# Second cross attention: the maxima are turned in fp32, and split into high and low part behind the turning, out of PSUM

## The reference

```python
x = x + _L0_attn_ref(_layernorm(x), ...)
x = x + _L0_xattn_ref(_layernorm(x), ctx_1024, fside_SxS2_0, ...)
x = x + _L0_ffn_ref(_layernorm(x), ...)
x = x + _L1_attn_ref(_layernorm(x), ...)
x = x + _L1_xattn_ref(_layernorm(x), ctx_1024, ctx_1024, ...)
x = x + _L1_ffn_ref(_layernorm(x), ...)
```

## Time and profile before

| | us |
|---|---|
| median of 3 runs | 1443.18 (1441.4 to 1446.35) |
| the profiled execution | 1440.46 |
| its span, first to last instruction | 1438.7 |
| granted TensorE clock over the span | 0.980 |
| batches 2 to 13 of the second cross attention | 26.95 each |

### The profile page before, as it was taken

One profiled execution on the slowest core, in us unless ns is written; L12 is line 12 of the kernel. 1 busy time (PEld: TensorE's weight loads), 2 busy tenths in 40 slices (PEclk: granted clock), 3 DMA queues, 4 the chain that ended last, 5 costly groups with the idle time before them and its releaser, 6 DMA issues.

```text
span 1438.7 us, 25389 instructions
## 1 busy us (share of the span) xinstructions
PE 1356.1 (94%) x9210; PEld 1010.9 (70%) x9210; DVE 1051.1 (73%) x2115; ACT 863.1 (60%) x1849; POOL 790.3 (55%) x442
## 2 busy tenths in 40 slices
PE   7889999999999999999999977999999999996898
PEld 4648888888888888888857654565565565553687
DVE  6558777888887788877735678677777777771687
ACT  4437666676766676666614444666666666653575
POOL 5036444433444444441452280788888888898363
PEclk9999999999999999999998999999999999998899
DMA  3122222221111222221230314463453463410231
GB/s 84 62 89 53 55 57 57 56 57 45 38 47 48 57 57 55 53 56 35 82 111 25 87 23 107 109 142 96 108 142 97 110 141 95 90 42 1 86 103 47
DMA packets 71803, 104.39 MB, mean 73 GB/s; under 512 B 14670, under 2 KB 54934, under 8 KB 71550
## 3 DMA queue, kind: packets, MB, share of 16 engines
q1 hardware_dynamic: 60062, 91.39, 25.4%
q10 hardware_dynamic: 11616, 11.38, 2.8%
HBM read 63.65 MB, written 2.11 MB: 46 GB/s over the span
## 4 chain that ended last, share of the span: by engine, by line
PE 80%; DVE 10%; DMA 3%; POOL 2%; ACT 2%; issue 2%; SPq 1%; ACTq 0%; POOLq 0%; DVEq 0%
PE PS L701 9%; PE PS L1100 6%; PE PS L715 6%; PE PS L689 5%; PE PS L690 5%; PE PS L691 5%; PE PS L717 5%; PE PS L716 5%; PE PS L1114 5%; PE PS L1080 5%; PE PS L1039 3%; PE PS L1045 3%; POOL QO_area L1220 2%; PE PS L1731 2%; DMA inv_kept<-row_inv 2%; DVE QO_area L1386 2%
## 5 line engine op out<-in xcount | busy, mean ns | idle before, releaser
L1220 POOL TENSOR_TENSOR QO_area<-QO_area,prob_a 125x896 f32<-125x896 f32 x160 | 335.8, 2098 | 24.1 <-ACT prob_a L1312 3.2
L867 ACT ACTIVATE HL<-PS 125x512 fp32r<-125x512 f32 (+1 forms) x384 | 206.6, 539 | 178.4 <-PE PS L701 161.2
L959 DVE TENSOR_TENSOR HL<-PS,HL 125x512 fp32r<-125x512 f32 (+1 forms) x384 | 238.1, 622 | 74.8 <-ACT HL L867 54.1
L1386 DVE TENSOR_REDUCE QO_area<-PS 112x1 f32<-112x500 f32 x384 | 239.1, 671 | 59.9 <-PE PS L1080 59.6
L1312 ACT ACTIVATE prob_a<-PS 125x448 f32<-125x448 f32 x384 | 187.5, 540 | 105.9 <-PE PS L1100 100.8
L774 POOL TENSOR_TENSOR HL<-ctx_area,ones 125x512 fp32r<-125x512 f32 (+1 forms) x64 | 93.0, 1453 | 246.7 <-PE PS L717 193.6
L715 PE MATMUL PS<-HL 125*128 125x512 f32 (+1 forms) x384 | 155.7, 405 | 2.5 <-DVE HL L959 1.7
L689 PE MATMUL PS<-HL 128*128 128x500 f32 x336 | 153.2, 456 | 4.1 <-DVE HL L929 4.0
L1100 PEld LDWEIGHTS PS<-HL 98*125 98x125 f32 x768 | 102.5, 186 | 71.9 <-ACT prob_a L1312 38.8
L877 ACT ACTIVATE prob_a<-prob_a,neg_max 128x500 f32<-128x500 f32 x192 | 135.5, 706 | 26.2 <-DVE neg_max L951 24.9
L1100 PE MATMUL PS<-HL 98*125 98x256 f32 x768 | 144.2, 309 | 1.6 <-ACT prob_a L1312 1.6
(11 more groups left out here) (260 smaller groups left out, 2729.3 us busy)
## 6 DMA issues: line engine op xcount, KB each, us to landing
HL<-prob_b SPq DMA_DIRECT2D x128, 187.5 KB, 4.0
ctx_area<-in_ctx_T SPq DMA_DIRECT2D x16, 750.0 KB, 13.0
ctx_area<-in_ctx SPq DMA_DIRECT2D x16, 750.0 KB
HL<-ctx_area SPq DMA_DIRECT2D x64, 187.5 KB, 3.8
inv_area<-in_ctx_T SPq DMA_DIRECT2D x8, 750.0 KB, 4.3
prob_a<-in_ctx_T SPq DMA_DIRECT2D x8, 750.0 KB, 4.6
inv_area<-inv_kept ACTq DMA_DIRECT2D x16, 256.0 KB, 3.3
ctx_area<-in_L_ffn_W SPq DMA_DIRECT2D x16, 256.0 KB, 3.2
```

Source lines behind the costliest of these rows:

```text
L867: nc.scalar.activation(pH[k % 3][0:KC, 0:width(g)], PS[0:KC, 2 + k % 3, 0:width(g)], ACT.Copy)\
L959: nc.vector.tensor_tensor(pL[k % 3][0:KC, 0:width(g)], PS[0:KC, 2 + k % 3, 0:width(g)], pH[k % 3][0:KC, 0:width(g)].bitcast(fp32), ALU.sub ...
L1220: nc.gpsimd.tensor_tensor(late_acc[b % 2], before, late_p[n % LATE_P], ALU.add).then_inc(m["padd"], 1)
L1386: nc.vector.tensor_reduce(late_part[b % 2][:, u // NKB, u % NKB:u % NKB + 1], PS[0:2 * S, u % NKB, 0:KB], AX, ALU.max).then_inc(m["mx"], 1)
```

## The change

`late_nmHL` goes, and with it the rounding and the subtraction ahead of the turning (lines 1395 and 1396). The fp32 maxima (112 x 8) are turned as they are, in step c = 0 instead of c = 1. ScalarE copies the turned 8 x 112 out of PSUM, rounded to fp32r, in step c = 0: this is the high row, and its DMA is issued there (`send_maxima(b, 0)`). In step c = 1, behind its two reductions, VectorE subtracts this high row from the PSUM original (`low_maxima`), and ScalarE, which waits for that (`nmlow`), issues the DMA of the low row behind its exponentials of c = 1. The key product of c = 2, which overwrites bank 7, waits for `nmlow` instead of `nmcopy`. The diff, without file names and unchanged neighbours:

```diff
         late_wq = carve(128, 4 * 3 * QUAD).rearrange("p (j r c) -> p j r c", j=4, r=3)
         late_nm = [carve(2 * S, 8) for i in range(2)]
         late_part = [carve(2 * S, 8 * NKB).rearrange("p (s w) -> p s w", s=8) for i in range(2)]
-        late_nmHL = [carve(2 * S, 16).bitcast(fp32r) for i in range(2)]
-        late_nmT = [carve(16, 2 * S).bitcast(fp32r) for i in range(2)]
+        late_nmT = [[carve(8, 2 * S).bitcast(fp32r) for r in range(2)] for i in range(2)]
         late_inv = [carve(128, 4 * S) for i in range(2)]
         late_p = [prob0[0:KC, i * HQ:(i + 1) * HQ] for i in range(LATE_P)]
         late_acc = [carve(KC, HQ) for i in range(2)]
...
         ld_k = [sem("ld_k0")]
         ld_late = [sem(f"ld_late{i}") for i in range(2)]
 
-        names = ("wqrep qp qhi qlo q0set qset ones kmm khi klo stack vmm vev mxmm mx nmsplit nmtr nmcopy nmrow "
+        names = ("wqrep qp qhi qlo q0set qset ones kmm khi klo stack vmm vev mxmm mx nmsplit nmtr nmcopy nmlow nmrow "
                  "sc exp pv padd sum norm wo out").split()
         la = {n: sem(f"late_{n}") for n in names}
         ld_v = sem("ld_v")
...
 
                 if piece == 0:
                     if b >= 2:
-                        pe.wait_ge(m["nmcopy"], b - 1)
+                        pe.wait_ge(m["nmlow"], b - 1)
                 elif piece < 4:
                     pe.wait_ge(m["khi"], 3 * b + piece)
                     pe.wait_ge(m["klo"], 3 * b + piece)
...
 
                 pe.wait_ge(m["nmsplit"], b + 1)
                 pe.wait_ge(m["vev"], 3 * min(b + 2, B))
-                nc.tensor.transpose(PS[0:16, 7, 0:2 * S], late_nmHL[b % 2].bitcast(fp32),
+                nc.tensor.transpose(PS[0:8, 7, 0:2 * S], late_nm[b % 2],
                                     ident[0:2 * S, 0:2 * S]).then_inc(m["nmtr"], 1)
 
             def scores(b, c, half):
...
                         project(b + 2, c - 2)
                     if b + 2 < B and c in (6, 8, 10):
                         project(b + 2, c // 2)
-                    if c == 1 and 0 <= b < B:
+                    if c == 0 and 0 <= b < B:
                         turn_maxima(b)
                     if 1 <= n:
                         product((n - 1) // NC, (n - 1) % NC)
...
                 act.wait_ge(m["nmtr"], b + 1)
                 if b >= 2:
                     act.wait_ge(m["nmrow"], 2 * 16 * (b - 1))
-                nc.scalar.activation(late_nmT[b % 2], PS[0:16, 7, 0:2 * S], ACT.Copy).then_inc(m["nmcopy"], 1)
+                nc.scalar.activation(late_nmT[b % 2][0], PS[0:8, 7, 0:2 * S], ACT.Copy).then_inc(m["nmcopy"], 1)
                 act.wait_ge(m["nmcopy"], b + 1)
                 act.wait_ge(m["ones"], 1)
                 if b >= 3:
                     act.wait_ge(m["sc"], 2 * NC * (b - 2))
-                for r in range(2):
-                    act.dma_start(
-                        late_q[b % 3].bitcast(fp32)[3 * QUAD + r:3 * QUAD + r + 1, 0:HQ],
-                        late_nmT[b % 2].bitcast(fp32)[8 * r:8 * r + 8, :]).then_inc(m["nmrow"], 16)
+                send_maxima(b, 0)
+
+            def send_maxima(b, r):
+
+                if r:
+                    act.wait_ge(m["nmlow"], b + 1)
+                act.dma_start(
+                    late_q[b % 3].bitcast(fp32)[3 * QUAD + r:3 * QUAD + r + 1, 0:HQ],
+                    late_nmT[b % 2][r].bitcast(fp32)).then_inc(m["nmrow"], 16)
 
             def first_keys():
                 for piece in range(3):
...
                         values(b + 2, c // 2 - 3, 7)
                     if b + 2 < B and c == 5:
                         queries(b + 2)
+                    if c == 0 and 0 <= b < B:
+                        place_maxima(b)
                     if c == 1 and 0 <= b < B:
-                        place_maxima(b)
+                        send_maxima(b, 1)
                 nc.scalar.preload_act_table(ACT.Sqrt)
 
             return first_keys, rest
...
                 dve.wait_ge(m["mx"], NKB * 8 * (b + 1))
                 if b >= 2:
                     dve.wait_ge(m["nmtr"], b - 1)
-                hl = late_nmHL[b % 2]
-                nc.vector.tensor_reduce(late_nm[b % 2], late_part[b % 2], AX, ALU.max, negate=True)
-                chain.link(dve, nc.vector.tensor_reduce(hl[:, 0:8], late_part[b % 2], AX, ALU.max, negate=True))
-                nc.vector.tensor_tensor(hl[:, 8:16], late_nm[b % 2], hl[:, 0:8].bitcast(fp32), ALU.subtract)\
+                nc.vector.tensor_reduce(late_nm[b % 2], late_part[b % 2], AX, ALU.max, negate=True)\
                     .then_inc(m["nmsplit"], 1)
+
+            def low_maxima(b):
+
+                dve.wait_ge(m["nmcopy"], b + 1)
+                if b >= 2:
+                    dve.wait_ge(m["nmrow"], 2 * 16 * (b - 1))
+                nc.vector.tensor_tensor(late_nmT[b % 2][1], PS[0:8, 7, 0:2 * S], late_nmT[b % 2][0].bitcast(fp32),
+                                        ALU.subtract).then_inc(m["nmlow"], 1)
 
             def normalise(b):
                 dve.wait_ge(m["sum"], b + 1)
...
                     if b + 1 < B:
                         maxima(b + 1, 2 * c)
                         maxima(b + 1, 2 * c + 1)
+                    if c == 1 and 0 <= b < B:
+                        low_maxima(b)
                     if b + 2 < B and c in (2, 3, 4):
                         keys(b + 2, c - 2, 7)
                     if n >= NC and n % NC == 3:
```

## The result

The changed kernel takes 1435.04 us, median of 8 runs (1431.6 to 1440.53), against 1444.24 us for the kernel before, median of 8 (1441.4 to 1449.36): ratio 0.9934, with a 95% interval of 0.9917 to 0.9951. By the ratio that is 9.5 us less (7.1 to 12.0), between the two medians 9.2 us; 6.9 us were forecast. The predicted time, 1436.3 us, is 1.3 us off. The profiled execution has a span of 1435.0 us at a mean clock of 0.975.

A forecast was written before the change was run, and what follows sets the result against it. TensorE bounds the kernel, stalled once a batch by VectorE's subtraction; GpSimd binds the end from batch 13. 12 x (1.07 - 0.43) = 7.7, less 0.5 and 0.3, is 6.9 us: 1443.18 to 1436.3 us, range 1430.5 to 1443.5.

The forecast's parts named there:

- Part 1: Steps c = 0 and c = 1: removing the subtraction ahead of the turning cuts 4.45 to 3.38 us, gaining 1.07 a batch.
- Part 2: VectorE's added 8 x 112 subtraction out of PSUM: 0.28 us, the middle of 0.18 and 0.391 us.
- Part 3: ScalarE's copy and first DMA issue moved from c = 1 to c = 0: exponentials 0.3 us late, cost nothing.
- Part 4: ScalarE's wait for nmlow before the second DMA issue delays TensorE's key product at c = 3: 0.43 us lost a batch.
- done at s + 0.94: Low row subtraction's end, in us after step c = 2 starts (s): reductions end s + 0.62, gap 0.04, subtraction 0.28.
- Part 5: Batches 0 and 1: batch 0 loses 0.5 us by the key product's wait; batch 1 gains nothing and loses 0.3 us.
- The end: From batch 13's first addition GpSimd runs 33 additions back to back, 2.227 us each; only gains before that move the end.
- The sum: Whole kernel: 12 x (1.07 - 0.43) = 7.7 us, less 0.5 and 0.3, gives 6.9 us gained.
- the rivals: Four other outcomes: wait at c = 3 takes nearly all (0.16), wait hidden (0.10), contention (0.07), stall stays (0.07).
- The slower one: VectorE behind c = 1's reductions: new subtraction waits for GpSimd, 1.83 us; 11.7 us slower, 1455 us; chance 0.07.

The follow-up runs named there:

- e1: The kernel before with the subtraction of line 1396 replaced by a third reduction, so the low row holds the high row again; ratio 0.9909.
- e2: The changed kernel run again without an edit, on the chip of e1, e3 and e4; ratio 0.9931 to the kernel before.
- e7: The changed kernel with the low row subtracted from an fp32 copy in SBUF, made by ScalarE, instead of out of PSUM; ratio 1.0041 to the kernel before.
- e5: The changed kernel with ScalarE's low row wait and second DMA issue moved behind the key copy of c = 2; ratio 0.9906 to the kernel before.
- e6: The changed kernel plus an unused 112 x 8 subtraction with two SBUF inputs at the old one's place on VectorE; ratio 1.0036 to the kernel before.
- e8: The changed kernel with the low row's subtraction done twice in a row; a single time, 1438.31 us.
- e4: e3 with the last batch's 11 additions done by VectorE instead of GpSimd; ratio 0.9874 to the kernel before.
- e3: The changed kernel with both DMAs of the maxima rows issued by SyncE instead of ScalarE; ratio 0.9905 to the kernel before.
- e9: e3 with the low row subtracted one step earlier, behind c = 0, in batch 0 alone; ratio 0.9901 to the kernel before.
- e10: e4 with batch 14's column sums and normalising moved behind all work of batch 15; ratio 0.9845 to the kernel before.

## Why the prediction was right

- *Part 1, the gain at c = 0 and c = 1:* 1.07 us forecast, 4.45 - 3.37 = 1.08 measured, and e1 gives the same from the instruction alone.
- *Part 2, the new subtraction:* 0.28 us forecast, 0.25 measured.
- *Part 3, ScalarE's copy and first issue at c = 0:* at no cost, and so it is. The exponentials of c = 1 started 0.73 us behind their scores instead of 0.54 (1003.88 for 1003.15), which nobody waited for.
- *Part 4, the wait for the low row:* the mechanism as forecast, step by step, and its size off: 0.43 us forecast, 0.28 measured (4.02 - 3.74), 0.25 in batch 4 alone (4.01 - 3.76). The term mis-sized is "done at s + 0.94": it was done at s + 0.79. I had let the subtraction begin a gap of 0.04 us behind the reductions' recorded end, but it begins 0.08 us ahead of it (1005.33, where the pair that starts at 1004.15 ends 1.26 us later), as the records of VectorE's instructions overlap there; the rest is the 0.03 us of the subtraction.
- *Part 5:* batch 1 cost 0.4 us (interval of the first additions 26.18 before, 26.59 after), 0.3 forecast. Batch 0 cost 1.6 instead of 0.5: the wait of 0.49 us was right, the clock under it was not foreseen.
- *The end:* 73.5 us from batch 13's first addition on, in every kernel with GpSimd's 33 additions, whatever was done to the batches before. This held exactly.
- *The sum:* 12 x 0.80 = 9.6 us, less 0.4 and 1.6, gives 7.6 us by the traces, where 6.9 were forecast; measured over all runs are 9.5 us (7.1 to 12.0), an interval that holds the 7.6 near its lower end. Two errors of mine, 12 x 0.16 = 1.9 us too little gain and 1.2 too little loss, partly cancel. That the predicted time is only 1.3 us off is partly luck too: it was counted from a median before of 1443.18 us, and that of all 8 runs is 1.06 us higher. Between profiled executions the time ahead of the stage, where nothing was changed, differs by up to 7 us (first split at 891.27 in e2, 898.72 in e7), so a single pair of spans (1438.7 and 1435.0) says less than the stage's own intervals.

Of the rivals, none happened. The slower one was real as a mechanism (e7) and did not apply as the operand lies in PSUM.

## What to carry to other kernels

A tiny VectorE instruction that takes ten times its time, and not always, is waiting for somebody: look at how many of its inputs lie in SBUF and at what GpSimd does beside it, and see whether one of them can be read from PSUM. When work is moved off the path, follow the new wait to the engine's next work: here a wait and an issue of ScalarE ahead of the exponentials of c = 2 gave 0.3 us of 1.1 back, and the same two behind the key copy (e5) cost nothing. And look how far a gain can travel: what is saved after the point where another engine has no idle time left does not arrive at the end.

## What the runs showed of the hardware

- A 112 x 8 subtraction with two SBUF inputs took 1915 ns on average beside GpSimd's additions of 2.10 us (e6), an 8 x 112 one 1181 ns (e7), and with one input in PSUM 253 to 257 ns (the change, e8). In batch 0, without additions, the first two took 159 and 254 ns. In the kernel before such a subtraction ended 0.02 to 0.04 us behind the end of an addition, in 15 batches of 15.
- VectorE's additions of 125 x 896 with two SBUF inputs hold up GpSimd's as well: 22 of these took 50.6 us beside two of VectorE's, 49.1 us alone (e4, e3).
- The granted clock of TensorE stayed at 0.50 (1.2 GHz) for 8 us in batch 0 of the change, after a wait of 1.55 us for a DMA and one of 0.49 us for the low row; without the second wait it was at 0.50 for some 3 us (before, e9). It stayed there for 16 us in e10, with the engine counted as busy throughout, after a stretch with 1.54 us without work.
